# Key projections first in the prologue, and another order at both ends of the experts

## What is computed

```python
x = x + _L0_xattn_ref(_layernorm(x), ctx_768, Wq, Wk, Wv, Wo, bo)
x = x + _L0_ffn_ref(_layernorm(x), router_w, w1, b1, w2, b2)
# _L0_xattn_ref
q, k, v = x @ Wq, context @ Wk, context @ Wv          # 16 heads of 64
attn = softmax(einsum('bqhd,bkhd->bhqk', q, k) / 8)
out = einsum('bhqk,bkhd->bqhd', attn, v) @ Wo + bo
# _L0_ffn_ref
scores = softmax(x @ router_w.T)
gate_vals, sel_idx = top_k(scores.T, 513)             # for each expert
h = gelu(x[sel_idx] @ w1[e] + b1[e])
y = (h @ w2[e] + b2[e]) * gate_vals
out = zeros.at[sel_idx].add(y)
```

## Time and profile before

| | us |
|---|---|
| median of three runs | 1386.02 |
| profiled execution | 1399.06 |
| its span, first to last instruction | 1397.3 |
| prologue block | 0 to 78.6 |
| search, lists and first gathers of the experts block | 1116.7 to 1163.2 |
| eight experts, to the last scatter row | 1163.2 to 1388.5 |
| TensorE busy | 1307.2 (94%) |
| VectorE, ScalarE, POOL busy | 1020.8, 805.9, 892.5 |

### The profile page before, as it was taken

How to read it: one execution, slowest core, us unless ns; L and a number is a source line. 1 busy time by engine, 2 the same in 40 slices (tenths; PEclk the granted TensorE clock), 3 DMA queues, 4 the chain that set the end, 5 groups by cost and what they waited for, 6 DMA issues and landing times. The chain is left out here.

```text
span 1397.3 us, 24897 instructions
## 1 busy us (share of the span) xinstructions
PE 1307.2 (94%) x8340; PEld 822.3 (59%) x8340; DVE 1020.8 (73%) x1670; ACT 805.9 (58%) x1090; POOL 892.5 (64%) x463
## 2 busy tenths in 40 slices
PE   6989999999999999999999999999899817999995
PEld 5655555555555555555555555555448817999995
DVE  5767877877877887787778778777776685655652
ACT  4556666666666666666566666666562215556552
POOL 2347876887786788778678877967683003455353
PEclk8999999999999999999999999999999857999998
DMA  9530010001001000100100010011315333444322
GB/s 269 181 128 9 24 55 18 17 24 56 21 20 58 17 17 24 56 24 17 58 17 17 24 56 24 16 47 69 112 37 181 109 122 121 117 122 104 93 40 24
DMA packets 75863, 88.83 MB, mean 64 GB/s; under 512 B 10555, under 2 KB 55644, under 8 KB 75740
## 3 DMA queue, kind: packets, MB, share of 16 engines
q1 hardware_dynamic: 68956, 78.32, 17.3%
q0 software_dynamic: 6784, 8.94, 4.0%
HBM read 58.98 MB, written 27.99 MB: 62 GB/s over the span
## 5 line engine op out<-in xcount | busy, mean ns | idle before, releaser
L917 POOL TENSOR_TENSOR acc_p<-acc_p,x_in 128x1024 f32<-128x1024 f32 x192 | 488.7, 2545 | 131.1 <-ACT x_in L1017 124.4
L100 DVE TENSOR_REDUCE mx_part<-ps_m 128x1 f32<-128x512 f32 x552 | 363.0, 685 | 182.3 <-PE ps_m L81 180.5
L1017 ACT ACTIVATE x_in<-ps_s 128x1024 f32<-128x1024 f32 x384 | 380.2, 1023 | 97.3 <-PE ps_s L833 70.2
L845 PE MATMUL ps_o<-x_in,v 128*64 128x512 f32 x1664 | 407.3, 607 | 0.5 <-DMA v<-v_scr 0.5
L822 PE MATMUL ps_s<-q,k 64*128 64x512 f32 x2496 | 386.1, 395 | 0.9 <-ACT x_in L1017 0.9
L822 PEld LDWEIGHTS ps_s<-q,k 64*128 64x128 f32 x2496 | 273.5, 185 | 41.7 <-ACT x_in L1017 6.6
L81 PE MATMUL ps_m<-k,q 64*128 64x512 f32 x736 | 212.1, 455 | 9.6 <-PEq L216 3.2
L845 PEld LDWEIGHTS ps_o<-x_in,v 128*64 128x64 f32 x1664 | 99.8, 136 | 182.1 <-issue 142.6
L81 PEld LDWEIGHTS ps_m<-k,q 64*128 64x128 f32 x736 | 99.8, 184 | 145.7 <-issue 102.3
L917 DVE TENSOR_TENSOR acc_d<-acc_d,x_in 128x1024 f32<-128x1024 f32 x96 | 176.5, 1839 | 5.9 <-ACT x_in L1017 5.5
L689 ACT ACTIVATE kept<-ps_m 128x512 f32<-128x512 f32 x184 | 109.7, 596 | 50.4 <-PE ps_m L81 47.7
(11 more groups left out here) (252 smaller groups left out, 1945.1 us busy)
## 6 DMA issues: line engine op xcount, KB each, us to landing
w_in<-in_w SPq DMA_DIRECT2D x16, 1024.0 KB, 5.0
v_st<-rec_scr SPq DMA_DIRECT2D x64, 128.0 KB, 2.9
o_scr<-v_st SPq DMA_DIRECT2D x32, 256.0 KB, 2.1
v<-v_scr SPq DMA_DIRECT2D x8, 832.0 KB, 5.2
v_scr<-c_in SPq DMA_DIRECT2D x10, 512.0 KB, 3.3
c<-o_scr SPq DMA_DIRECT2D x2, 1792.0 KB, 7.6
x_in<-in_x SPq DMA_DIRECT2D x4, 512.0 KB, 10.7
k<-o_scr SPq DMA_DIRECT2D x1, 2048.0 KB, 8.0
```

Source lines behind the costliest of these rows:

```text
L100: dve.tensor_reduce(part[:, j // S.MF, j % S.MF:j % S.MF + 1], bank[:, 0:S.MC], AX.X, ALU.max).then_inc(done or G.rough_used[hd], 1)
L845: last = pe.matmul(ps_o[hd * HP:hd * HP + DH, :], v[b][:, s, hd * DH:(hd + 1) * DH], probs[:, g % RING, hd * QC:(hd + 1) * QC], start=(s = ...
L917: eng.tensor_tensor(acc, other, probs[:, (u * KT + t) % RING, :], ALU.add).then_inc(done, 1)
L1017: act.activation(probs[:, g % RING, :], ps_s[:, g % 2, :], ACT.Exp, bias=G.pad_bias[:, 0:1] if s == KT - 1 else 0.0, scale=SCALE).then_inc ...
```

## The change

Prologue:
- The 128 columns of Wk of the first pair of heads are loaded by three DMAs on ScalarE's queue at the start; SP loads the other 896 columns where it loaded all before. SP waits for `s_eps` in place of `s_cz`.
- The key projections stand right behind the context turns. Then come twelve value jobs v0 to v11 (`VX = 12`) where there were eight, then the turns of x, each pair with one value job (v12 to v15 in place of v8 to v11) and the query projections as before.
- ScalarE splits Wk's first pair ahead of the context, Wv's second half between the key projections, and the rest of Wk behind the copy of v3. POOL's order follows.
- The row of maxima stands ahead of v25 in place of v23, and the rough jobs behind v17 to v25.

Experts:
- The slices of w1's low part begin in round 4 of the search; what is left (640 columns) stands behind the masks, ahead of the wait for the prefix sums.
- Expert 0's tiles are turned in two groups, tiles 0 to 2 and tile 3 with the tail. The first column half of h 0 stands between them and that of h 1 behind them.
- In the last expert the turns of tiles 0 and 1 stand inside the third y job, in place of behind the third and the fourth.
- SP, not POOL, waits for the last scatters. The semaphore `masks_set` is merged into `consts`.

```diff
@@ prologue, ScalarE
+                load_split(act, 0, "wk", pair0, s_wk0)
                 act.wait_ge(s_eps, 1)
                 act.activation(std[:, 0:1], eps[:], ACT.Sqrt).then_inc(s_eps, 1)
+                weight_hi(0, pair0, s_wk0, 48)
                 for j in range(NC):
                     hi(j)
                 weight_hi(2, half0, s_wv[0], 48)
...
                 proj_hi(0)
                 proj_hi(1)
+                weight_hi(2, half1, s_wv[1], 48)
                 proj_hi(2)
                 proj_hi(3)
+                for n in range(4):
+                    keep_v(n)
+                weight_hi(0, pairs, s_w[0], 48)
+                for n in range(4, 7):
+                    keep_v(n)
...
@@ prologue, TensorE
-                for n in range(4):
-                    values(n)
-                proj(0)
-                proj(1)
-                values(4)
-                proj(2)
-                proj(3)
-                for n in range(5, 8):
+                for n in range(NPJ):
+                    proj(n)
+                for n in range(VX):
                     values(n)
...
@@ experts, TensorE
+            if first:
+                pe_first_xgt(pe, 0)
+                pe_h(pe, 0, b, 0, (0,))
+                pe_first_xgt(pe, 1)
+                pe_xgt(pe, 0, 0, 0, TJ - 1)
+                pe_h(pe, 0, b, 1, (0,))
             for h in range(HT):
-                pe_h(pe, e, b, h)
+                pe_h(pe, e, b, h, (1,) if first and h < 2 else (0, 1))
...
+                if last_expert and n == 2 and h in LAST_TURN:
+                    pe_turn(pe, e, LAST_TURN[h])
...
-        LO_ROUND, LO_COLS = ROUNDS - 8, S.HID // 8
+        LO_ROUND, LO_COLS = 4, S.HID // 8
...
@@ experts, SP
+                for b in range(2):
+                    sp.wait_ge(scattered[b], 16 * ST * (E // 2))
@@ experts, POOL
-                for b in range(2):
-                    pool.wait_ge(scattered[b], 16 * ST * (E // 2))
```

More of the change, by code:

```diff
@@ L140, in phase_prologue @@
         CG = -(-KT // 4)
-        s_c, s_cz = [sem(f"p_c_loaded{i}") for i in range(CG)], sem("p_c_padded")
+        s_c, s_wk0 = [sem(f"p_c_loaded{i}") for i in range(CG)], sem("p_wk0_loaded")
         s_x = [sem(f"p_x_loaded{i}") for i in range(4)]
@@ L174, in phase_prologue @@
         half0, half1, pair0, pairs = slice(0, S.DI // 2), slice(S.DI // 2, S.DI), slice(0, P), slice(P, S.DI)
[L175 to L180, removed]
+        K0_HI, V_HI, K_HI, Q0_HI, Q_HI = 1, 3, 4, 5, 6
+        K0_LO, V1_LO, K_LO, Q0_LO, Q_LO = 1, 2, 3, 4, 5
+        VX, VR = 12, 17
+        BANK_USE = ("k0 k1 k2 k3".split() + [f"v{n}" for n in range(VX + 1)] + "v13 q0 v14 q1 v15 q2 v16 q3".split()
+                    + [f"v{n}" for n in range(VR, len(vjobs) - 1)] + ["mx"] + [f"v{n}" for n in range(len(vjobs) - 1, len(vjobs))])
+        ROUGH_BEHIND = {17: (3,), 18: (4,), 19: (5, 6), 20: (7, 8), 21: (9,), 22: (10, 11), 23: (12,), 24: (13,), 25: (14,)}
         ROUGH_LAST = (15, 16)
@@ L229, in _ @@
                              A["ctx"][0, (KT - 1) * P:S.NK, P:S.DC]).then_inc(s_c[CG - 1], 16)
[L231 to L239, removed]
+                load_split(sp, 2, "wv", half0, s_wv[0])
+                load_split(sp, 2, "wv", half1, s_wv[1])
+                load_split(sp, 0, "wk", pairs, s_w[0])
                 for g in range(4):
@@ L432, in _ @@
                 act.activation(std[:], mv[:, :, 1], ACT.Sqrt, bias=eps[:, 0:1]).then_inc(s_std, 1)
-                for n in range(5, 8):
+                for n in range(7, VX):
                     keep_v(n)
@@ L528, in _ @@
                     turn(NC + 2 * g + 1)
[L529 removed]
+                    values(VX + g)
                     if g >= 2:
@@ L1544, in phase_experts @@
         gathered = [sem(f"gathered{b}") for b in range(2)]
-        first_gathered = [sem(f"first_gathered{n}") for n in range(2)]
+        first_gathered = [sem(f"first_gathered{n}") for n in range(3)]
         def got(b, n):
@@ L1641, in pool_gather @@
             for j in range(ST):
-                done = first_gathered[j // 2] if first and j < ST - 1 else gathered[b]
+                done = first_gathered[max(j - 1, 0)] if first and j < ST - 1 else gathered[b]
                 pool.indirect_dma_start(xg[b][:, j, :], None, G.table,
@@ L1668, in pe_xgt, with pe_first_xgt @@
                 r = rows[j]
-                last = pe.transpose(ps_t[:, bank, c * RT:c * RT + r], xg[b][0:r, j, k * P:(k + 1) * P], G.ident[0:r, 0:r])
+                out = tail_bank(e) if n == TJ - 1 else ps_t[:, bank, :]
+                last = pe.transpose(out[:, c * RT:c * RT + r], xg[b][0:r, j, k * P:(k + 1) * P], G.ident[0:r, 0:r])
             last.then_inc(xgt_ready, 1)
-        def pe_first_xgt(pe):
-            for j in range(ST - 1):
-                if j % 2 == 0:
-                    pe.wait_ge(first_gathered[j // 2], 32)
+        FIRST_TILES = (slice(0, 3), slice(3, ST - 1))
+        def pe_first_xgt(pe, n):
+            tiles = FIRST_TILES[n]
+            for j in range(tiles.start, tiles.stop):
+                if j != 1:
+                    pe.wait_ge(first_gathered[max(j - 1, 0)], 32 if j == 0 else 16)
                 for k in range(KD):
                     last = pe.transpose(ps_t[:, k, j * RT:(j + 1) * RT], xg[0][0:RT, j, k * P:(k + 1) * P], G.ident[0:RT, 0:RT])
-                    if j == ST - 2:
-                        last.then_inc(xgt_ready, 1)
-            pe.wait_ge(gathered[0], got(0, 1))
-            pe_xgt(pe, 0, 0, 0, TJ - 1)
+            last.then_inc(xgt_ready, 1)
         def act_xgt(act, e, n):
             act.wait_ge(xgt_ready, TJ * e + n + 1)
-            src, hi, _ = xgt_views(n)
+            src, hi, _ = xgt_views(e, n)
             act.activation(hi, src, ACT.Copy).then_inc(xgt_hi_done, 1)
@@ L1703, in pe_h @@
             terms = [(w, x, k) for k in range(KD) for w, x in ((w1_hi[b], xt_hi), (w1_hi[b], xt_lo), (w1_lo[b], xt_hi))]
-            for c in range(2):
+            for c in halves:
                 for n, (w, x, k) in enumerate(terms):
@@ L1818, in pe_expert @@
                         pe_xgt(pe, e + 1, *nxt(i, b), m)
-                if n >= 2:
+                if n >= 2 and not last:
                     pe_turn(pe, e, n - 2)
```

116 lines of the change are left out of this document (59 added, 57 removed).

## The result

Laid against runs of the kernel before on the same chip, the changed kernel takes 1.0025 times as long (95% interval 1.0018 to 1.0033), from medians of 1391.38 and 1387.83 us: **3.5 us slower**, between 2.5 and 4.6. The forecast was +1.1 us and no change that can be told. The time lies inside the range of 1382.0 to 1391.5 us, by 0.1 us, and partly by a base that came out 1.8 us above the 1386.02 us from which the forecast started. The chain of waits came as predicted; the size was 2.4 us short. Two of the twenty executions of the changed kernel took 2942.3 and 1839.3 us; they are left out of the ratio, and nothing here shows why they took so long.

The account below looks back on a forecast made before the run. TensorE, busy for 94% of the span, was taken as the bound, so only its idle or low-clock stretches count. Prologue +5.3, experts' start -1.5, scatter 2 -0.8 and drain -1.9 gave +1.1 us: 1387.1 us, range 1382 to 1391.5.

Parts of the forecast that it names:

- The chain of the stall: Prologue: v8's copy waits for value tile 0's store behind the key stores; third turn of x at 42.1 us, 4.4 later.
- The gap and the clock: Prologue, before the third turn of x: TensorE idles over 6 us, the clock falls and 2.0 us are lost.
- Before ... the next turn of x at 37.72 us: Prologue: the old third turn of x, used as base against the new 42.1 us, giving 4.4 us later.
- 1.1 us won: Prologue, q3 to the attention block: 24.7 us against 25.8, so 1.1 us won.
- Prologue in all: Whole prologue: +4.4 + 2.0 - 1.1 = +5.3 us, bounds +2 and +7.5.
- Start of the experts: Search to expert 0: first half of h 0 starts at 1161.0 instead of 1163.22 us; -1.5 us, between -0.6 and -2.0.
- Scatter 2: End, last expert: with two turns moved into the third y job, scatter 2 starts at 1382.7 us, -0.8 us.
- Drain: End: with the wait on SP, POOL's drain starts with its last scatter row and ends 1.9 us earlier, bounds 0 and -2.
- The clock rival: Prologue's x rounds: clock stays low, two more rounds at 1.2 GHz cost 3 to 4 us, giving 1391 us; chance 10%.

Follow-up runs that it names:

- The edit of SP's order: Changed kernel with the stores of value tiles 0 to 3 ahead of the four key weight stores on SP's queue: ratio to before 0.9935.
- the two new ones: Profiles of the changed kernel (1.0025) and of the kernel before with only the prologue's part of the change (1.0055, 7.6 us slower).
- the six old ones: Six profiles with the old prologue: two of the kernel before, one each with both experts' ends, experts' start, last turns, SP's wait; attention starts at 77.19 us on average.
- the second profile of before: The kernel before, unchanged, profiled again because the first profile took 13 us more than the median: ratio 0.9998.
- the three parts of the experts: Kernel before with one experts part each: start 0.9986, two turns moved into the last expert's third y job 0.9996, SP's wait for the scatters 0.9988.
- The ends run together: Kernel before with all of the change in the experts on the old prologue: ratio 0.9960, 5.5 us faster.
- the profile of the experts' start: Kernel before with only the start of the experts changed (w1's low part in the search, turns in two parts, h in halves): 0.9986, 1.9 us faster.
- SP's wait alone: Kernel before with only the wait for the scatters moved from POOL to SP: 0.9988, 1.7 us faster.

## Why the prediction was right or wrong

- **The chain of the stall: right.** Five times in a row (high part, low part, first key store, copy of v8, third turn of x) came within 0.5 us. The edit of SP's order shows that the late store was the cause.
- **The gap and the clock: right.** From the third turn of x to q3's last pair it takes 16.4 us now (41.65 to 58.09) and 14.5 in the earlier trace rows (37.72 to 52.19): 2.0 us more, as predicted; 1.4 from the mean of the two new ones to that of the six old ones. The granted clock is back at 46.4 us, after 4.7 us of half-speed work in that stretch.
- **"Before ... the next turn of x at 37.72 us": this is the term that was mis-sized most.** The row is right, but it is that of the latest of six executions. It holds a loss of clock from 29 us to 34.8 us that only one other of the six has. I even read that loss, and used it to price the new gap, without asking whether it belongs to every execution. Against the mean of six, 35.85 us, the new turn (41.65 and 42.00) comes 6.0 us later, not 4.4. At q3 and at the start of the attention the row's profile is 1.4 and 1.5 us behind the mean, so this base took 1.5 us out of the sum. How much of the 1.5 us is the clock is not shown: the second profile of before, without the loss, is 1.4 us earlier, and the others vary by other waits as well.
- **"1.1 us won" after q3: mis-sized.** From q3's last pair to the attention it is 26.0 us in the two new prologues (84.1 - 58.1) and 26.4 in the mean of the old ones: 0.4 us; between the two traces first shown it is 0.2. I had the right row for the wait behind Wq's stores. But ScalarE's late copy then held TensorE for 2.16 us, the clock fell once more (0.50 from 78 to 80 us), the last value job ran at 1.2 GHz, and the copy of v25 began only at 79.64 us.
- **Prologue in all:** +5.3 predicted, inside bounds of +2 to +7.5; 7.6 us timed (6.0 to 9.3), 6.9 by the traces. Between the two traces first shown it is 5.7 (84.36 - 78.65): 3.9 to the third turn, 2.0 for the clock, 0.2 won. That this is so near to 5.3 is in part luck, as the term for the third turn was 0.5 too high and that behind q3 0.9 too hopeful.
- **Start of the experts:** -1.5 predicted, -1.9 timed, -2.0 by the two traces laid side by side. Inside the bounds. The first h matmul came 2.2 us nearer to the gathers, as worked out.
- **Scatter 2:** -0.8 predicted, -0.75 measured, with the turns' cost in it.
- **Drain:** -1.9 predicted, -1.7 timed, 2.0 in the trace. The page of the Trainium skill that I had weighed for this (Perfetto Trace Analysis, DMA Instruction — SWDGE (GPSIMD)) has the row end with the last descriptor; the trace agrees, as SP sees the data landed 1.8 us behind the end of POOL's last row.
- **The sum of single runs:** +7.6 for the prologue and -4.2 for the three parts of the experts give +3.4, and the whole change gives +3.5. The ends run together (-5.5) would give +2.1, within the intervals.

The clock rival, at 10%, would have given 1391 us, and the median is 1391.38. That is chance: its two further rounds at 1.2 GHz did not come, as the clock was back at 46.4 us, within the first round of x behind the gap.

## What to carry to other kernels

A stage that gets ahead of its consumers runs into the next thing that must come free, and here that was a staging slot behind unrelated stores in one FIFO of transfers. Move the order of the stores together with the order of the work: alone, the new order of the work made this kernel slower and the new order of the stores brought nothing; both together made it faster. And before a stretch of one trace serves as the base of a sum, look whether its clock fell there, and whether it also falls in a second profile of the same kernel; a duration at the lower clock is a price for that loss, not a property of the stretch.

## What the runs showed of the hardware

The same instructions behind the same wait ran at either level of the clock. In the old prologue a wait of 1.58 us was followed by 3.7 us at 1.2 GHz in the profile of the experts' start, and the same wait of 1.58 us by none in the second profile of before. Near 980 us, in the attention, TensorE waits for 1.8 us and, after some 2 us of work, for up to 1.8 us again. The granted clock falls there in eleven of the fourteen profiles and not in the three others. One of these, SP's wait alone, has the same instructions up to there as the kernel before; first the second profile of before, then that of SP's wait alone:

```profile
984.00:986.00 2.00, 2.00 (x8) 0.47 (x4) 0.07 (x1) 0.31 (x1) 1.62 (x1) 0.50 0.00 0
```

```profile
984.00:986.00 2.00, 2.00 (x13) 0.90 (x11) 0.56 (x2) 0.77 (x3) 1.58 (x1) 1.00 0.00 0
```

From the start of the attention to the threshold's transpose behind the search it takes 1066.0 us in the first and 1064.9 in the second, and 1065.9 to 1067.7 us in all eleven profiles with the fall against 1064.8 to 1065.1 in the three without it. So a part of the scatter of single times goes with this one event, about 1 us between the two shown. The Trainium skill (TensorE: Matmul & The Clock Gate, Part 1) says of the slow matmuls at the start of a kernel that their number is "run-variable". The traces here show the like for a gap in the middle of one.

The granted clock of the windows can miss a slow stretch: in the second profile of before it reads 1.00 from 15 to 20 us, where single value matmuls take 0.63 us each, as they do at 0.50, and not 0.39.

POOL's drain at the end takes 6.6 us (6599 ns) in each of the profiles in which POOL waits for the scatters first, and ends 6.6 us behind its last indirect scatter row where nothing stands between; the drains of the other engines there take 0.01 to 0.52 us.
